# Moving the first image's reconstruction ahead of the odd set's correlation, and the next round's even scan ahead of image 1's coefficients

## What is computed

```python
x = x + _L0_conv_ref(_gn(x), ...)      # group norm (one channel a group), then two ternary 3x3 convolutions, one gated
x = x + _L1_conv_ref(_gn(x), dictionary)
```

```python
G = D.T @ D + DIAG_EPS * I
h_bar = (D.T @ X).T                      # correlation of every patch with every atom
for k in range(1, 6):
    index = argmax(abs(h * ~mask))       # the pick of this step
    # a small triangular system over the picks so far -> x_stack
    h = h_bar - x_stack @ G[I]           # the correlation is updated with rows of G
coeffs[I] = x_stack
X_hat = D @ coeffs                       # the image is reconstructed from its atoms
```

## Time and profile before

| | |
|---|---|
| time, median of 3 runs | 532.79 us (530.71 to 532.8) |
| profiled execution | 535.74 us, span 533.7 us |
| TensorE (PE) | 429.4 us busy, 80% of the span |
| VectorE (DVE) | 447.4 us, 84% |
| ScalarE (ACT) | 317.7 us, 60% |
| GpSimdE (POOL) | 147.5 us, 28% |
| mean granted TensorE clock | 0.942 of full speed |

### The profile page before, as it was taken

The page is one execution under the profiler, slowest core; times in us unless marked ns, Lnnn a source line. Parts: engine busy times, 40 slices in busy tenths (PEclk is TensorE's granted clock), DMA queues, the critical chain, the costliest instruction groups (busy, mean ns, idle before and its releaser), DMA issues.

```text
span 533.7 us, 7983 instructions
## 1 busy us (share of the span) xinstructions
PE 429.4 (80%) x1948; PEld 324.7 (61%) x1948; DVE 447.4 (84%) x2268; ACT 317.7 (60%) x712; POOL 147.5 (28%) x162
## 2 busy tenths in 40 slices
PE   0089974999885869999894979999958897988685
PEld 0033862556665755557774864568757776867574
DVE  4665668888899959978999889998999999989983
ACT  2535448856558359866697299757740754456340
POOL 3000044433300153532300355443000764430010
PEclk9999997999889887999997899999997999989798
DMA  5999712899300043999510174521400665224256
GB/s 99 176 143 151 139 40 72 139 168 147 68 1 1 9 101 89 161 177 174 119 41 1 29 168 112 132 64 47 83 1 1 158 153 133 68 67 88 47 109 128
DMA packets 110206, 50.76 MB, mean 95 GB/s; under 512 B 103632, under 2 KB 104144, under 8 KB 110160
## 3 DMA queue, kind: packets, MB, share of 16 engines
q1 hardware_dynamic: 99480, 25.60, 29.8%
q0 software_dynamic: 8160, 24.13, 19.6%
q10 hardware_dynamic: 2520, 0.53, 0.5%
HBM read 34.24 MB, written 8.65 MB: 80 GB/s over the span
## 4 chain that ended last, share of the span: by engine, by line
PE 50%; DVE 29%; ACT 8%; issue 6%; SPq 3%; another core or an unknown queue 1%; DMA 1%; DVEq 0%; ACTq 0%
PE h L391 30%; PE conv_ps L391 15%; DVE junk L1062 9%; PE back_ps L391 6%; DVE top L992 3%; SPq L261 3%; DVE top_i L1007 2%; DVE top_i L1005 2%; ACT diag L683 2%; ACT score L674 2%; DVE coef L1203 2%; DVE mask L1089 2%; ACT xb L640 1%; ACT xa L640 1%
## 5 line engine op out<-in xcount | busy, mean ns | idle before, releaser
L363 POOL DMA_INDIRECT rows<-gram,idx_u x128 | 129.1, 1009 | 329.3 <-DVEq L1049 299.2
L391 PE MATMUL h<-rows,diag 128*128 128x256 f32 x640 | 152.3, 395 | 26.0 <-ACT diag L683 22.0
L391 PEld LDWEIGHTS h<-rows,diag 128*128 128x128 f32 x640 | 123.9, 197 | 54.9 <-issue 37.5
L1062 DVE SCALAR_TENSOR_TENSOR junk<-mask,rows 128x256 bf16<-128x256 bf16 x320 | 119.1, 417 | 0.0
L683 ACT ACTIVATE diag<-ident,dx 128x128 f32<-128x128 f32 x320 | 96.8, 388 | 34.8 <-DVEq L1156 33.0
L674 ACT ACTIVATE score<-h 128x512 f32<-128x512 f32 x80 | 47.0, 596 | 97.4 <-PE h L391 85.6
L992 DVE MAX8 top<-score 128x8 f32<-128x256 f32 x160 | 65.1, 418 | 34.5 <-ACT score L674 30.4
L391 PE MATMUL h<-d_sb,z 128*128 128x256 f32 x256 | 68.2, 431 | 23.7 <-DVEq L983 23.7
L391 PEld LDWEIGHTS h<-d_sb,z 128*128 128x128 f32 x256 | 63.5, 329 | 28.7 <-DVEq L983 25.4
L391 PE MATMUL conv_ps<-xa,w_taps 128*64 128x512 f32 x128 | 62.6, 612 | 4.0 <-DVEq L1267 4.0
L391 PE MATMUL conv_ps<-xb,w_taps 128*64 128x512 f32 x128 | 62.6, 612 | 0.0
(11 more groups left out here) (156 smaller groups left out, 569.2 us busy)
## 6 DMA issues: line engine op xcount, KB each, us to landing
xa<-in_x SPq DMA_DIRECT2D x64, 128.0 KB
out<-x SPq DMA_DIRECT2D x60, 128.0 KB, 2.7
x<-y POOLq DMA_DIRECT2D x14, 512.0 KB
xb<-in_x SPq DMA_DIRECT2D x48, 128.0 KB, 4.9
rows<-gram,idx_u POOLq DMA_INDIRECT x128
xb<-in_x SPq DMA_DIRECT2D x16, 120.0 KB, 5.3
d_sb<-in_L_conv_dictionary SPq DMA_DIRECT2D x4, 128.0 KB, 3.9
out<-x ACTq DMA_DIRECT2D x4, 128.0 KB
```

Of the source, the lines that this page charges most:

```text
L363: pool.indirect_dma_start(out=rows[s][:, k, t, :], out_offset=None, in_=gram_dram[:, :], in_offset=bass.IndirectOffsetOnAxis(ap=idx_u[s][: ...
L391: return nc.tensor.matmul(dst, lhs, rhs, start=start, stop=stop, skip_group_check=skip)
L1062: c = step(v.scalar_tensor_tensor(out=place, in0=mask_of(r, s, k, t), scalar=1.0, in1=source, op0=ALU.mult, op1=ALU.mult, accum_out=dst))
```

## The change

TensorE: in `body`, `coef_transposes(b, 0)` and `reconstruct(b, 0)` stand ahead of `correlate(r, 1)` and `x_sums(f)`. ScalarE: `copy_coef(b, 0)` stands ahead of the next round's `x_statistics` and of `scores(r, 1, 0)`. VectorE: `body` hands the odd set's last `solve` to the next round's even scan, which now comes at once behind what is left of `spread(r, 0)`; the set's `select` and `solve` follow, laid between `spread(r-1, 1)`, and then `restart` and the odd scan. The amount of arithmetic is the same.

```diff
@@ TensorE, body @@
-                correlate(r, 1)
-                if front:
-                    x_sums(f)
                 if behind:
                     coef_transposes(b, 0)
                     reconstruct(b, 0)
+                correlate(r, 1)
+                if front:
+                    x_sums(f)
                 update(r, 0, 0)
@@ ScalarE, body @@
+                if behind:
+                    copy_coef(b, 0)
                 if front and behind:
                     for m in range(IMG_R):
                         x_statistics(f, m)
                 scores(r, 1, 0)
-                if behind:
-                    copy_coef(b, 0)
@@ VectorE, all_picked and body @@
-                after(picked_h[s])
+                if picked_h[s]:
+                    after(picked_h[s])
...
-            def body(r, front, behind):
+            def body(r, front, behind, last_solve=iter(())):
                 f = r + 1
-                restart()
-                junk_n[0] = 0
                 nothing = iter(())
-                chain = [nothing, nothing]
+                chain = [nothing, last_solve]
...
-                    if k:
-                        scan(r, 0, k, together(chain[1], beside[0]), 1)
-                    else:
-                        scan(r, 0, k)
+                    scan(r, 0, k, together(chain[1], beside[0]), 1 if k else None)
                     select(r, 0, k, rows_of)
                     chain[0] = solve(r, 0, k)
                     extract(r, 0, k, chain[0])
+                    if k == 0:
+                        if behind:
+                            run(chain[0], spread(r - 1, 1))
+                        restart()
+                        junk_n[0] = picked_h[0] = 0
                     scan(r, 1, k, together(chain[0], beside[1]), 0)
...
                 all_picked(1)
-                run(chain[1], rows_of)
-                if front:
-                    run(spread(r, 1))
-
-            body(0, True, False)
+                run(rows_of)
+                return chain[1]
+
+            last_solve = body(0, True, False)
             for r in range(1, ROUNDS - 1):
-                body(r, True, True)
-            body(ROUNDS - 1, False, True)
+                last_solve = body(r, True, True, last_solve)
+            run(body(ROUNDS - 1, False, True, last_solve))
```

More of the change, by code:

```diff
@@ L542, in body @@
                 idle_bank = conv_ps[:, 1, 0:ATOMS] if behind else back_ps[1][:, 0, :]
+                if behind:
+                    coef_transposes(b, 0)
+                    reconstruct(b, 0)
                 correlate(r, 1)
@@ L545, in body @@
                     x_sums(f)
-                if behind:
-                    coef_transposes(b, 0)
-                    reconstruct(b, 0)
                 update(r, 0, 0)
```

## The result

The changed kernel is slower: 552.98 us median (549.82 to 554.89, four runs) against 531.75 (529.18 to 532.8, four runs), a ratio of 1.040 with a 95% interval of 1.033 to 1.047. The forecast was 551.2. The profiled execution took 554.9 with a span of 552.8, against a forecast of 554.1.

What follows compares the result with a forecast made beforehand. Bound: the chain over each round boundary from T through odd correlation, C, odd scores, normalization, norm_x and diagonals to the update. Boundaries of 4.5, 6.9 and 7.0 gave +18.4 us on a 532.8 median: 551.2, range 542.5 to 558.

Steps and rivals of the forecast that it cites:

- Order of TensorE's list, the large term: TensorE: the odd correlation waits behind image 0's work, ending 8.3, 7.2 and 7.9 us later at the three boundaries.
- C: End of the odd correlation on TensorE; forecast at T + 17.7, against T + 9.4, 10.5 and 9.8 before.
- T: Moment when VectorE's last pick out of h1 releases TensorE; 291.90 at the second boundary before the change.
- Statistics on ScalarE costed at nothing: ScalarE: statistics behind the waiting copy end at T + 12.7, ahead of C at T + 17.7; cost nothing.
- Even scan, 4.5 us earlier, costed at nothing: VectorE: even scan starts at about T + 1.3 instead of T + 5.8; neither gain nor loss.
- First boundary: C 8.3 us later, less 3.8 won back from a ScalarE stall of 3.94: 4.5 us slower.
- Second boundary: C 7.2 us later, less 0.3 because norm_x no longer stands behind out_back: 6.9 us slower.
- Third boundary: C 7.9 us later, less 0.9 of VectorE's wait for even scores: 7.0 us slower.
- The price of a further fall: Rival: TensorE's clock falls behind C, image 1's reconstruction 2.4 us longer at second boundary; in full 26 us, 559; chance 0.06.
- The gap is filled: Rival: image 0's work fills TensorE's 7.0 us gap, clock stays up; about 6 us faster, 527; chance 0.07.
- No change: Rival: TensorE's list behind C is as critical as C, a later wait swallows the delay; 533; chance 0.05.
- The clock stays up: Rival: TensorE's clock stays up, C at the low bound T + 14.4; 7.4 us slower, 540; chance 0.10.

Runs made afterwards that it cites:

- change again: The changed kernel, unaltered, run once more for a second profile (also called its second profile): 547.15 us.
- the ninth kernel: TensorE and ScalarE as in the change, image 0's coefficients ahead of the picks, VectorE otherwise in before's order: 530.45 us, 1.009 to before.
- first pair: The first profiles of before and of the change: spans 533.7 and 552.8 us.
- second pair: The profiles of before again and change again: spans 522.9 and 545.0 us.
- before again: The kernel before, unaltered, run once more for a second profile: 525.02 us.
- the fourth kernel: The change, but VectorE completes image 0's coefficients ahead of the odd set's last picks: 525.92 us, 0.991 to before.
- VectorE's part alone: The change with TensorE's and ScalarE's order put back to that of before: 526.97 us, 0.993 to before.
- the fifth kernel: The change with 13 spare matmuls on TensorE ahead of image 0's transposes: 546.36 us, 1.027 to before.
- the first group: The first four experiments, with their own runs of before, median 530.2 us.
- the third group: The experiments after the first eight, also called the last group, with their own runs of before, median 525.3 us.
- the first two groups: The first four experiments and the next four, with runs of before at medians of 530.2 and 531.3 us.
- the second and the eighth experiment: Second: before with only TensorE's and ScalarE's reordering, 547.62 us, 1.036. Eighth: the change with 6 and 5 more spare matmuls in the last round, 548.71 us, 1.034.
- experiments 1, 3, 4, 5 and 7: 1, 4, 5: VectorE's part alone, the fourth kernel, the fifth kernel. 3: the change, statistics ahead of copy, 551.17 us. 7: fourth kernel with spare matmuls, 524.94 us.

## Why the prediction was right, and where it was off

*Order of TensorE's list, the large term.* Right. C was forecast at T + 17.7 and came at T + 16.7, 17.8 and 16.8 (T taken as the start of the three coefficient instructions), and in the second profile at 17.1, 18.4 and 17.1. VectorE's old order with TensorE's new one has the whole loss, and VectorE's new order alone none. The pieces: 1.3 for the coefficients (1.27 busy), 1.9 for the cold half of the transposes (2.08), 0.7 for the copy (0.69 idle), 6.1 for the reconstruction (5.10, 6.16 and 5.17), 7.7 for the correlation (7.63). So the reconstruction was a microsecond too dear at the first and third boundaries, and right at the second.

*Statistics on ScalarE costed at nothing.* Right: 8.8 us behind the copy, over ahead of the scores' release, and moving them back changed nothing. The margin was smaller than the 5 us from T + 12.7 to C: the first half of the scores is released 3.7 us ahead of C, and waited only 1.24 us.

*Even scan, 4.5 us earlier, costed at nothing.* Right for this change. It is not a fact about the scan: the ninth kernel shows that it becomes a price as soon as C moves forward and its cover goes.

*First boundary.* The mechanism was right and the term mis-sized. I gave back 3.8 us for a stall of before that I took for a part of the kernel. In the first pair of profiles the give-back was larger still (the reconstruction of image 1, cold behind the stall in before, was 5.36 for 6.11, and norm_x came 6.4 behind C), and the stage grew by 0.4 only; without the stall, in the second pair, it grew by 7.0. Before took 117.07 us for this stage with the stall and 110.15 without, so 3.94 us of stall came with 6.9 us of time: TensorE idled behind it, and the transposes (3.75 for 1.95) and the reconstruction (6.11 for 3.72) then ran at the lower clock. The change had two stalls in the same stage, of 2.71 and 3.36 us at 230.52 and 252.04, and took 117.49 with them and 117.13 without. Stalls of like length did not cost alike. Without that term the sum would have been 8.0 + 6.9 + 7.0 = 21.9, against 22.1 in the undisturbed pair and 21.2 between the first medians.

*Second boundary.* Forecast 6.9, measured 7.2, and 9.0 in the second pair, where before's odd correlation took 9.27 for 10.51 because its clock rose sooner, and the change's reconstruction 6.75 for 6.16.

*Third boundary.* Forecast 7.0, measured 10.1 and 5.4. The rows of TensorE show where the two part:

| third boundary, us behind T | before | change | before again | change again |
|---|---|---|---|---|
| even update of step 2 starts | 47.3 | 54.8 | 46.9 | 54.0 |
| its duration | 5.42 | 7.10 | 7.11 | 5.42 |
| end of the span | 130.9 | 141.0 | 132.2 | 137.6 |

Up to this update the change is 7.5 and 7.1 us later, as forecast. The update itself ran at the lower clock for longer in the change of the first pair and in before of the second, which adds 1.7 to the one difference and takes 1.7 from the other. The scatter is the clock's. The price of a further fall I had placed behind C at the second boundary; it came there (5.41 for 3.72 us) without moving the odd update, since the diagonal was awaited to nearly the same time, and in the first profile it came in the last round, where I had none, at 3.0 us for one update, of which the change again shows half.

*Luck.* The first pair of spans differs by 19.1 us, close to the 18.4 forecast, but not by the terms of the sum: 4.1 less than forecast at the first boundary, 0.3 more at the second, 3.1 more at the third, and 1.4 us ahead of any boundary, where the kernels do the same work. The second pair, without stalls, is 3.7 above the sum and bears out its mechanism better.

*The rivals.* "The gap is filled" failed in the change for the reason given, coefficients behind T, and held once they stood ahead of the picks. I had put its worth at 6 us; the fourth kernel was 4.3 below before in its group, but VectorE's part alone, with the gap left open, was 3.2 below, so what the filled gap is worth is not shown. "No change" failed, as C was waited for on both other engines. "The clock stays up" did not happen, and the fifth kernel, which aimed at it, kept the clock up only for the transposes at the first two boundaries, and for the reconstruction too at the third.

What stays open is what ScalarE waits for in the stalls, and whether VectorE's order makes them fewer. Before was 0.7% slower than VectorE's part alone in the first group, where three of four profiles have stalls; with fillers added to that part, it was 0.2% slower in the third group, where none has. That the difference is the stalls is an argument and not shown.

## What to carry to other kernels

Work is moved into an engine's idle gap only if its last input is ready ahead of the event that ends the gap: in an in-order list, a wait that ends 1.3 us behind that event put 8 to 9 us of work in front of the critical product. So look for the instruction that completes the input first. Here, three of them stood behind the picks, and moving them turned 1.040 into 0.991.

What is costed at nothing because other work covers it should be priced again in every version in which that cover has moved. And before a stall goes into a sum, a second profile should show that it belongs to the kernel.

## What the runs showed of the hardware

ScalarE's unnamed waits of 2.7 to 3.9 us came up to three times in one execution: 18 in the ten profiles of before, the change and the first two groups, with none in the second and the eighth experiment, and none in the four profiles of the last group. The kernel before had a median of 525.3 us there, and of 530.2 and 531.3 in the other two groups. Their places are not wholly chance: 17 of the 18 stand ahead of a half of `scores`, and in six profiles (the change and experiments 1, 3, 4, 5 and 7) one stands at 101.6 to 102.5 us. A difference of 1% between kernels of different groups is therefore no finding, and they are compared above by their ratios.

TensorE's clock also fell where the engine had no long idle stretch ahead of it. The fifth kernel, second boundary, behind 5.78 us of filler (columns as in the earlier trace rows):

```profile
294.00:296.80 2.80, 1.16 (x8) 0.97 (x8) 2.62 (x12) 0.63 (x2) 0.00 (x0) 0.87 0.00 0
296.80:303.00 6.20, 6.18 (x15) 4.94 (x16) 5.80 (x24) 6.20 (x11) 2.70 (x3) 0.51 0.12 30
```

No idle time there was over 1.94 us, and yet the granted clock was 0.51, the 1.2 GHz level, for nearly the whole reconstruction, which took 6.72 us instead of 3.72.

The same sequence need not end so. At the third boundary of the same execution TensorE did the same work with the same idle times, and the clock stayed up:

```profile
412.66 1.16 PE L391 MATMUL back_ps<-ident,coef 128*128 128x128 f32 x8 [1.94 <-DVEq L1211]
414.50 3.72 PE L391 MATMUL back_ps<-coef_t,d_t 128*128 128x256 f32 x16 [0.69 <-ACT coef_t L691]
```

The three reconstructions of this execution took 5.36, 6.72 and 3.72 us. A term of a sum that hangs on the clock is therefore a range, and one profile gives one value out of it.
